# A multiply of the scan's inputs, from VectorE to GpSimd: a decoder layer with a selective scan on one core

## The chip, the cores and the metric

The kernel runs on one core of a Trainium2 chip. The metric is the device time of one execution in microseconds (us); lower is better. The engines are TensorE (PE in the profile, its weight loads PEld), VectorE (DVE), ScalarE (ACT), GpSimd (POOL) and SyncE (SP), which here only issues DMAs. SBUF and PSUM are the on-chip memories; GpSimd works on SBUF only.

## What is computed

One layer with three parts, each with a residual and a layer norm, for x of 4 batch rows x 512 positions x 512 channels, in float32. The change lies in the first part, a selective scan over 1024 inner channels (e) with 16 states (n) each:

```python
hidden = silu(conv(x @ W_in[:, :E]) + conv_bias)           # b, e, l
dt, Bm, Cm = split(hidden^T @ W_x, [128, 144])             # 128 + 16 + 16
dts = softplus(dt @ W_dt + b_dt)                           # b, l, e
dA  = exp(dts[..., None] * A)                              # b, l, e, n
dBu = dts[..., None] * Bm[:, :, None, :] * hidden[..., None]
state = dA[t] * state + dBu[t];  y[t] = sum_n state * Cm[t]
out = ((y + hidden * D) * silu(gate)) @ W_out
```

Behind it come an attention over a context (softmax) and a feed-forward product on values rounded to int8 range.

## The kernel before

Everything is written by hand for each engine, with semaphores between them. The batch rows are worked one after the other, each as 32 steps g (`STEPS`, with the row b from -1 to 4; -1 prepares row 0, 4 finishes row 3). A tile of 128 inner channels (8 per row) is scanned in four **units** of 32 channels x 4 states on the 128 partitions, each with 4 states more along the free axis (`NJ`). Step g of row b works unit u = 32 b + g + 1. Positions run along the free axis, 512 of them.

What a tile needs goes as follows. TensorE makes z = dt_s @ W_dt for the tile (item "z", at steps with g % 4 == 2, two tiles ahead: `Z_AT`). ScalarE's `soft` (L523 to L532) writes softplus of it to `steps[:, n % 3, 0]` and raises `s_dt`. `step_inputs` (L724 to L734) multiplies it with the convolved input `hs` into `steps[:, n % 3, 1]` and raises `s_du`. SyncE's `repeat` (L342 to L349) waits for `s_du` and copies 32 rows of both, four times over, into one of four `rep` buffers for each unit. From `rep`, ScalarE's `exps` make dA (four activations a unit, one unit ahead).

VectorE's `unit(u)` (L736 to L758) does two **products** dBu = rep * Bb, each 128x1024, from SBUF to PSUM (L747), then, at two units of lag (`DU_LAG`) behind the z item, the multiply `step_inputs` (L733), then two **scans** over dA in SBUF and dBu in PSUM (L755) into `st`. GpSimd's `weigh_states(u, h)` (L428 to L437) multiplies each half of the states with C, in place. Half 0 waits for the first scan of the unit. Half 1 waits for the second scan, and also for the products of the next unit and for the multiplies that stand behind them:

```python
if h and u + 1 < NB * UNITS:
    pool.wait_ge(s_mul, NH * (u + 2))
    pool.wait_ge(s_du, step_inputs_before(u + 2))
```

TensorE sums the weighted states of four units over partitions (`state_sum`, L886, at g % 4 == 0), VectorE's `finish` (L719) multiplies with the gate at g % 4 == 1. The products, attention and feed-forward of the row before are spread over the same steps (`REST`): layer-norm operations on VectorE (L700), small operations on GpSimd (L450, L452, and the bias add L461 of 128x512). `items(b, g)` lists the work of a step, and each engine goes through it in that order.

Of the kernel before, what the change touches and what calls it, by code (L numbers as in the profile page):

```python
# [5 lines left out]
ALU = mybir.AluOpType  # L6
# [11 lines left out]
NE = E // P  # L18
# [4 lines left out]
NQ = 4  # L23
# [3 lines left out]
UNITS = NE * NQ  # L27
TT = T // P
BANKS = 4
REPS = 4  # L30
# [27 lines left out]
SUM_AT = 0  # L58
FINISH_AT = 1
AHEAD = 4  # L60
DU_LAG = 2
NORM_LAG = 1
QUANT_LAG = 2

# [4 lines left out]
def items(b, g):  # L69

    keys = []
    after = b + 1 < NB
    n = NE * b + g // 4
    table = REST_AFTER if b == NB else REST

    def rest(kb, table, kinds):  # L80
        for kind in kinds:
            keys.extend((kind, kb, i) for i, at in enumerate(table.get(kind, ())) if at == g)

    if after and g == (B_AT if b >= 0 else 27):
        keys.extend(("sb", b + 1, j) for j in range(NJ))
    if after and b >= 0:
        keys.extend(("sc", b + 1, j) for j, at in enumerate(C_AT) if at == g)
    if (b, g) == (-1, 28):
        keys.extend(("sc", b + 1, j) for j in range(NJ))
    if b >= 1:  # L90
        rest(b - 1, table, ("wo", "q", "k", "at", "en"))
    if (g % 4 == Z_AT and 0 <= n + 2 < NB * NE and n != -1) or (b, g) == (-1, 28):
        keys.append(("z", (n + 2) // NE, (n + 2) % NE))
    if after and b >= 0:
        keys.extend(("c", b + 1, i) for i, at in enumerate(CONV_AT) if at == g)
    if after:
        keys.extend(("h", b + 1, i) for i, at in enumerate(HID_AT) if at == g)
    if b >= 1:
        rest(b - 1, table, ("xt", "av", "qt", "ff"))
    if b == LAST:  # L100
        rest(b, REST_BESIDE, ("q", "k", "at", "en", "wp"))
    if after and g == DT_AT:
        keys.append(("dt", b + 1, 0))
    if after and g == (BC_AT if b >= 0 else DT_AT):
        keys.append(("bc", b + 1, 0))

    if g % 4 == GATE_AT and 0 <= n < NB * NE:
        keys.append(("g", n // NE, n % NE))
    if b == 0 and g in (1, 2):
        keys += [("w", 0, 2 * (g - 1)), ("w", 0, 2 * (g - 1) + 1)]  # L110
    if b == 0 and g == 4:
        keys.append(("ws", 0, 0))
    if g % 4 == SUM_AT and 0 <= n - 1 < NB * NE:
        keys.append(("y", (n - 1) // NE, (n - 1) % NE))
    return keys


STEPS = [(b, g) for b in range(-1, NB + 1) for g in range(UNITS)]


def step_inputs_at(u):

    s = UNITS + u - 1 - DU_LAG
    return [key for key in items(*STEPS[s]) if key[0] == "z"] if u >= 1 else []


def step_inputs_before(u):

    return sum(key[0] == "z" for b, g in STEPS[:max(UNITS + u - 1 - DU_LAG, UNITS)] for key in items(b, g))


def norm_order():
# [4 lines left out]
def decoder_layer(nc, x, xT, ctxT, w_in, w_conv, conv_k, conv_b, w_x, w_dt, b_dt, w_out, a_log, d_skip,  # L137
# [9 lines left out]
    with ExitStack() as ctx:  # L147
# [28 lines left out]
        hs = sb("hs", [P, 2, NE, T])  # L176
        steps = sb("steps", [P, 3, 2, T])
# [77 lines left out]
        s_hs = sem("hs_ready")  # L255
# [154 lines left out]
        @block.gpsimd  # L410
        def _(pool):
            for dst in (ident, sel):
                nc.gpsimd.memset(dst[:], 0.0).then_inc(s_maskset, 1)
            nc.gpsimd.memset(ones[:], 1.0).then_inc(s_masks, 1)
            nc.gpsimd.memset(unround[:], -ROUND).then_inc(s_masks, 1)
            nc.gpsimd.memset(rounder[:], ROUND).then_inc(s_masks, 1)
            nc.gpsimd.memset(eps[:], EPS).then_inc(s_masks, 1)
            nc.gpsimd.memset(neghalf[:], -0.5).then_inc(s_maskset, 1)
            pool.wait_ge(s_maskset, 3)
            nc.gpsimd.affine_select(out=ident[:], in_=ident[:], compare_op=ALU.not_equal, fill=1.0,  # L420
                                    base=0, pattern=[[-1, P]], channel_multiplier=1).then_inc(s_masks, 1)

            for n, d in enumerate(range(-3, 4)):
                if n:
                    pool.wait_ge(s_masks, 5 + n)
                nc.gpsimd.affine_select(out=sel[:], in_=sel[:], compare_op=ALU.not_equal, fill=1.0,
                                        base=32 * d, pattern=[[-1, P]], channel_multiplier=1).then_inc(s_masks, 1)
            def weigh_states(u, h):  # L428

                spread_read(pool, "sc", u, h)  # L430
                pool.wait_ge(s_scan, NH * u + h + 1)
                if h and u + 1 < NB * UNITS:
                    pool.wait_ge(s_mul, NH * (u + 2))
                    pool.wait_ge(s_du, step_inputs_before(u + 2))
                j = slice(JH * h, JH * h + JH)
                s = st[:, u % RING, j, :]
                nc.gpsimd.tensor_tensor(s, s, Cb[:, j, :], ALU.mult).then_inc(s_p, 1)  # L437

            rows = []
            for b, g in STEPS:  # L440
                u = UNITS * b + g + 1
                scanned = 0 <= u < NB * UNITS
                if scanned:
                    weigh_states(u, 0)
                for key in rows:

                    n = norm[key]
                    c = slice(n % 4, n % 4 + 1)
                    pool.wait_ge(s_var, n + 1)
                    nc.gpsimd.tensor_tensor(rstd[:, c], var[:, c], neghalf[:], ALU.pow).then_inc(s_rstd, 1)  # L450
                    pool.wait_ge(s_rstd, 2 * n + 1)
                    nc.gpsimd.tensor_tensor(nmean[:, c], nmean[:, c], rstd[:, c], ALU.mult).then_inc(s_rstd, 1)  # L452
                rows = []
                for key in items(b, g):
                    kind, kb, i = key
                    if kind == "qt":

                        pool.wait_ge(s_xq, TT * kb + i + 1)
                        pool.wait_ge(s_bias, 16 * min(kb + 1, LAST))
                        x_i = rows_of[kb][:, i, :]  # L460
                        nc.gpsimd.tensor_tensor(x_i, x_i, bias_bc, ALU.add).then_inc(s_xb, 1)  # L461
                    if key in norm:
                        rows.append(key)
                if scanned:
                    weigh_states(u, 1)
# [211 lines left out]
        def _(dve):  # L677
# [43 lines left out]
                dve.wait_ge(s_y, NE * b + e + 1)  # L721
                dve.sem_inc(free, 1)  # L722

            def step_inputs(key):  # L724

                _, b, e = key
                n = NE * b + e
                dve.wait_ge(s_dt, n + 1)
                dve.wait_ge(s_hs, n + 1)
                if n >= 3:  # L730
                    for v in range(NQ * (n - 3), NQ * (n - 2)):
                        dve.wait_ge(s_rep[v % REPS], 64 * (v // REPS + 1))
                V.tensor_tensor(steps[:, n % 3, 1, :], steps[:, n % 3, 0, :], hs[:, b % 2, e, :],  # L733
                                ALU.mult).then_inc(s_du, 1)  # L734

            def unit(u):  # L736
                dve.wait_ge(s_rep[u % REPS], 64 * (u // REPS + 1))
                if u >= RING:

                    n = (u - RING) // NQ  # L740
                    product_done(dve, ("y", n // NE, n % NE))
                for h in range(NH):
                    j = slice(JH * h, JH * h + JH)
                    spread_read(dve, "sb", u, h)
                    if u:
                        dve.wait_ge(s_scan, NH * (u - 1) + h + 1)
                    V.tensor_tensor(dBu[:, j, :], rep[:, u % REPS, 1:2, :].to_broadcast([P, JH, T]), Bb[:, j, :],  # L747
                                    ALU.mult).then_inc(s_mul, 1)
                for key in step_inputs_at(u):
                    step_inputs(key)  # L750
                for h in range(NH):
                    j = slice(JH * h, JH * h + JH)
                    dve.wait_ge(s_mul, NH * u + h + 1)
                    dve.wait_ge(s_dA, NJ * u + JH * (h + 1))
                    V.tensor_tensor_scan(st[:, u % RING, j, :].rearrange("p j t -> p (j t)"),  # L755
                                         dA[:, u % 2, j, :].rearrange("p j t -> p (j t)"),
                                         dBu[:, j, :].rearrange("p j t -> p (j t)"), 0.0,
                                         ALU.mult, ALU.add).then_inc(s_scan, 1)  # L758
# [23 lines left out]
            for s, (b, g) in enumerate(STEPS):  # L782
                if 0 <= UNITS * b + g + 1 < NB * UNITS:
                    unit(UNITS * b + g + 1)
                if b == -1:
                    for key in items(b, g):
                        if key[0] == "z":
                            step_inputs(key)
                if b == -1 and g == HID_AT[-1] + 1:
                    quantize_weight()  # L790
                n = NE * b + g // 4 - 1
# [245 lines left out]
```

## Time and profile before

| | |
|---|---|
| median of 3 runs | 1140.06 us (1139.74 to 1140.76) |
| profiled execution | 1141.5 us, span 1139.7 us |
| TensorE busy | 855.1 us (75%) |
| VectorE busy | 1015.2 us (89%) |
| ScalarE busy | 775.5 us (68%) |
| GpSimd busy | 688.5 us (60%) |
| granted TensorE clock, mean | 0.886 |

The span runs from the first to the last instruction. Busy times are sums over each engine; "idle before" is the time in which an engine waited ahead of an instruction, with the instruction that ended it. "issue" means that the profile shows nothing that it waited for. Instructions of one engine overlap by some hundredths of a microsecond.

### The profile page before, as it was taken

Reading aid. Unit: us, or ns where it says so; the run is one execution under the profiler, and the core shown is the slowest. Engines: PE = TensorE matmul, PEld = TensorE weight load, DVE = VectorE, ACT = ScalarE, POOL = GpSimd, SP = SyncE. Lnnn points to the kernel's source line nnn. Section 1 sums busy time; section 2 is a strip of 40 time slices with the busy share of each in tenths; the row PEclk is TensorE's granted clock in tenths of the full one; section 3 lists DMA queues with packets and bytes.
Section 4 is the critical chain, followed back from the end, with each engine's and each line's share of the span. In section 5 each row is a group of like instructions: output and inputs, shape, how many; then the busy total and the mean of one; then the engine's idle time right before and its main releaser. Section 6 shows DMA issues by size and latency. Waiting matters only on the chain.

```text
span 1139.7 us, 10601 instructions
## 1 busy us (share of the span) xinstructions
PE 855.1 (75%) x2958; PEld 335.9 (29%) x2968; DVE 1015.2 (89%) x813; ACT 775.5 (68%) x1193; POOL 688.5 (60%) x387
## 2 busy tenths in 40 slices
PE   7944578884689689987669689897569557757884
PEld 3311133331134233432124234332124223322331
DVE  3589999999989987999999988999989999999823
ACT  3466566775766776886666786886657777777446
POOL 1046666666666665777667655587656767677423
PEclk9978799997789899999789899999779768888996
DMA  6163344453732443343743443254733353243000
GB/s 183 45 155 87 92 121 117 114 138 104 190 98 63 114 117 94 100 117 93 215 120 83 111 109 103 59 141 112 216 89 74 95 136 84 57 133 97 1 0 38
DMA packets 58427, 120.09 MB, mean 105 GB/s; under 512 B 12160, under 2 KB 18432, under 8 KB 58368
## 3 DMA queue, kind: packets, MB, share of 16 engines
q1 hardware_dynamic: 57648, 119.34, 40.3%
q8 instruction: 24, 0.39, 0.1%
q14 instruction: 35, 0.29, 0.1%
q10 hardware_dynamic: 720, 0.08, 0.0%
HBM read 48.07 MB, written 4.19 MB: 46 GB/s over the span
## 4 chain that ended last, share of the span: by engine, by line
issue 39%; DVE 31%; PE 20%; ACT 7%; POOL 1%; DMA 1%; DVEq 0%; ACTq 0%; SPq 0%; POOLq 0%
DVE st L755 21%; PE dense L854 11%; DVE dBu L747 3%; PE dense L909 3%; PE dense L886 2%; DVE x L700 2%; ACT dA L542 2%; PE dense L933 1%; DVE hs L719 1%; DVE steps L733 1%; ACT L530 1%; DVE xsc L806 1%; DVE dense L838 1%; ACT squares L566 1%; ACT L519 1%
## 5 line engine op out<-in xcount | busy, mean ns | idle before, releaser
L437 POOL TENSOR_TENSOR st<-st,Cb 128x1024 f32<-128x1024 f32 x256 | 597.3, 2355 | 405.5 <-issue 236.4
L755 DVE TENSOR_TENSOR_SCAN st<-dA,dBu 128x1024 f32<-128x1024 f32 x256 | 570.2, 2268 | 0.0
L542 ACT ACTIVATE dA<-rep,Aneg 128x511 f32<-128x511 f32 x512 | 329.2, 712 | 88.2 <-DVE st L755 86.4
L747 DVE TENSOR_TENSOR dBu<-rep,Bb 128x1024 f32<-128x1024 f32 x256 | 327.6, 1323 | 21.9 <-issue 7.3
L854 PE MATMUL dense<-xTs,Win 128*128 128x512 f32 x512 | 239.3, 612 | 16.6 <-DVEq L722 8.2
L886 PE MATMUL dense<-st,sel 128*32 128x512 f32 x1024 | 125.3, 628 | 32.7 <-POOL st L437 32.4
L854 PE MATMUL dense<-wide,hs 128*128 128x512 f32 x256 | 121.9, 633 | 31.6 <-issue 31.6
L854 PEld LDWEIGHTS dense<-xTs,Win 128*128 128x128 f32 x512 | 98.7, 196 | 147.7 <-issue 147.0
L909 PE MATMUL dense<-pj,Win 128*128 128x512 f32 (+1 forms) x192 | 97.3, 654 | 28.9 <-issue 13.1
L542 ACT ACT_TABLE_LOAD x62 | 79.5, 1283 | 12.8 <-DVE st L755 7.4
L871 PE MATMUL dense<-ident,small 128*128 128x128 f32 x112 | 22.4, 337 | 82.4 <-ACT small L584 55.5
L854 PEld LDWEIGHTS dense<-wide,hs 128*128 128x128 f32 x256 | 51.1, 204 | 100.6 <-issue 100.3
L886 PEld LDWEIGHTS dense<-st,sel 128*32 128x32 f32 x1024 | 30.2, 113 | 123.5 <-issue 76.5
L450 POOL TENSOR_TENSOR rstd<-var,neghalf 128x1 f32<-128x1 f32 x48 | 44.2, 921 | 37.0 <-ACT var L569 36.7
L933 PE MATMUL dense<-small,sel 128*32 128x512 f32 x256 | 38.2, 717 | 37.8 <-DVEq L722 35.1
L576 ACT ACTIVATE x<-x,nmean,rstd 128x512 f32<-128x512 f32 x36 | 29.1, 816 | 51.6 <-POOL nmean L452 51.3
L909 PEld LDWEIGHTS dense<-pj,Win 128*128 128x128 f32 x192 | 39.0, 212 | 85.2 <-issue 78.0
L854 PE MATMUL dense<-wide 128*128 128x512 f32 x96 | 46.5, 630 | 0.3 <-issue 0.3
L871 PEld LDWEIGHTS dense<-ident,small 128*128 128x128 f32 x112 | 15.7, 169 | 98.9 <-ACT small L584 63.3
L700 DVE SCALAR_TENSOR_TENSOR x<-dense,x 128x512 f32<-128x512 f32 x36 | 24.7, 686 | 22.0 <-PE dense L854 15.7
L854 PE MATMUL dense<-dt_s,Wdt 128*128 128x512 f32 x64 | 39.5, 702 | 3.5 <-ACT dt_s L547 2.0
L637 ACT ACTIVATE ta<-dense 128x512 f32<-128x512 f32 x32 | 19.1, 598 | 33.0 <-PE dense L854 32.4
(105 smaller groups left out, 772.9 us busy)
## 6 DMA issues: line engine op xcount, KB each, us to landing
rep<-steps SPq DMA_DIRECT2D x512, 128.0 KB, 2.4
Win<-w_in SPq DMA_DIRECT2D x64, 256.0 KB, 2.9
wide<-w_out SPq DMA_DIRECT2D x4, 2048.0 KB, 10.3
Win<-w_conv SPq DMA_DIRECT2D x24, 256.0 KB, 2.9
xTs<-xT SPq DMA_DIRECT2D x4, 1024.0 KB, 5.5
x<-x SPq DMA_DIRECT2D x3, 1024.0 KB, 8.9
out<-x SPq DMA_DIRECT2D x12, 256.0 KB, 2.0
wide<-w_x SPq DMA_DIRECT2D x4, 640.0 KB, 4.9
```

Of the source, the lines that this page charges most:

```text
L437: nc.gpsimd.tensor_tensor(s, s, Cb[:, j, :], ALU.mult).then_inc(s_p, 1)
L450: nc.gpsimd.tensor_tensor(rstd[:, c], var[:, c], neghalf[:], ALU.pow).then_inc(s_rstd, 1)
L542: nc.scalar.activation(dA[:, u % 2, j, 1:T], rep[:, u % REPS, 0, 1:T], ACT.Exp, scale=Aneg[:, u % UNITS, j:j + 1]).then_inc(s_dA, 1)
L576: nc.scalar.activation(x_i, x_i, ACT.Identity, scale=rstd[:, n % 4:n % 4 + 1], bias=nmean[:, n % 4:n % 4 + 1]).then_inc({"wo": s_ln1, "av" ...
L700: V.scalar_tensor_tensor(x_i, ps, 1.0, x_i, ALU.mult, ALU.add, accum_out=rowsum[:, n % 4:n % 4 + 1]).then_inc(s_sum, 1)
L747: V.tensor_tensor(dBu[:, j, :], rep[:, u % REPS, 1:2, :].to_broadcast([P, JH, T]), Bb[:, j, :], ALU.mult).then_inc(s_mul, 1)
L755: V.tensor_tensor_scan(st[:, u % RING, j, :].rearrange("p j t -> p (j t)"), dA[:, u % 2, j, :].rearrange("p j t -> p (j t)"), dBu[:, j, :] ...
L854: mm = nc.tensor.matmul(ps[0:rows, :], lhsT, rhs, start=n == 0, stop=n == len(pairs) - 1)
L871: mm = nc.tensor.transpose(ps[:, k * P:(k + 1) * P], src[:, k * P:(k + 1) * P], ident[:])
L886: mm = nc.tensor.matmul(ps[32 * q:32 * q + 32, :], sel[:, 0:32], st[:, (4 * n + q) % RING, j, :], start=False, stop=j == NJ - 1)
L909: mm = nc.tensor.matmul(ps[:, k:T], Win[:, n % 3, k, :], pj[:, 0:T - k], start=k == 0, stop=k == KC - 1)
L933: mm = nc.tensor.matmul(ps[32 * n:32 * n + 32, :], sel[:, row + n:row + n + 1].to_broadcast([P, 32]), bc_s, start=True, stop=True)
```

## The change

The multiply leaves VectorE's program. GpSimd does it in the step whose items hold the z, between its weighing of half 0 and of half 1 of that step's unit, and behind the norm operations that stand there in some steps. The wait for loads of `rep` that stood ahead of it and GpSimd's wait for `s_du` are gone.

```diff
-DU_LAG = 2
...
             def weigh_states(u, h):
...
                 if h and u + 1 < NB * UNITS:
                     pool.wait_ge(s_mul, NH * (u + 2))
-                    pool.wait_ge(s_du, step_inputs_before(u + 2))
...
                 for key in items(b, g):
                     kind, kb, i = key
-                    if kind == "qt":
+                    n = NE * kb + i
+                    if kind == "z":
+
+                        pool.wait_ge(s_dt, n + 1)
+                        pool.wait_ge(s_hs, n + 1)
+                        nc.gpsimd.tensor_tensor(steps[:, n % 3, 1, :], steps[:, n % 3, 0, :], hs[:, kb % 2, i, :],
+                                                ALU.mult).then_inc(s_du, 1)
+                    elif kind == "qt":
...
-            def step_inputs(key):
-
-                _, b, e = key
-                n = NE * b + e
-                dve.wait_ge(s_dt, n + 1)
-                dve.wait_ge(s_hs, n + 1)
-                if n >= 3:
-                    for v in range(NQ * (n - 3), NQ * (n - 2)):
-                        dve.wait_ge(s_rep[v % REPS], 64 * (v // REPS + 1))
-                V.tensor_tensor(steps[:, n % 3, 1, :], steps[:, n % 3, 0, :], hs[:, b % 2, e, :],
-                                ALU.mult).then_inc(s_du, 1)
...
-                for key in step_inputs_at(u):
-                    step_inputs(key)
```

GpSimd's order around the first z of the scanned part, before: the weighings of units 2 and 3 and of half 0 of unit 4. The waits in brackets are semaphores: `scan_done`, `dBu_done` (a product), `step_inputs_ready` (the multiply).

```order
L437 TENSOR_TENSOR st<-st,Cb 128x1024 [waits scan_done]
L437 TENSOR_TENSOR st<-st,Cb 128x1024 [waits step_inputs_ready,dBu_done,scan_done]
L437 TENSOR_TENSOR st<-st,Cb 128x1024 [waits scan_done]
L437 TENSOR_TENSOR st<-st,Cb 128x1024 [waits step_inputs_ready,dBu_done,scan_done]
L437 TENSOR_TENSOR st<-st,Cb 128x1024 [waits scan_done]
```

And with the change (`steps_ready` is softplus, `hs_ready` the convolved input):

```order
L424 TENSOR_TENSOR st<-st,Cb 128x1024 [waits scan_done]
L424 TENSOR_TENSOR st<-st,Cb 128x1024 [waits dBu_done,scan_done]
L424 TENSOR_TENSOR st<-st,Cb 128x1024 [waits scan_done]
L448 TENSOR_TENSOR steps<-steps,hs 128x512 [waits hs_ready,steps_ready]
L424 TENSOR_TENSOR st<-st,Cb 128x1024 [waits dBu_done,scan_done]
L424 TENSOR_TENSOR st<-st,Cb 128x1024 [waits scan_done]
```

The multiply stands between the two weighings of unit 3, ahead of the one that waits for the products of unit 4.

VectorE's order, units 4 and 5 and the products of unit 6, before:

```order
L747 TENSOR_TENSOR dBu<-rep,Bb 128x1024 [waits scan_done,rep_loaded0]
L747 TENSOR_TENSOR dBu<-rep,Bb 128x1024 [waits scan_done]
L755 SCALAR_TENSOR_TENSOR st<-dA,dBu 128x1024 [waits dA_ready,dBu_done] x2
L747 TENSOR_TENSOR dBu<-rep,Bb 128x1024 [waits scan_done,rep_loaded1]
L747 TENSOR_TENSOR dBu<-rep,Bb 128x1024 [waits scan_done]
L733 TENSOR_TENSOR steps<-steps,hs 128x512 [waits hs_ready,steps_ready]
L755 SCALAR_TENSOR_TENSOR st<-dA,dBu 128x1024 [waits dA_ready,dBu_done] x2
```

With the change:

```order
L729 TENSOR_TENSOR dBu<-rep,Bb 128x1024 [waits scan_done,rep_loaded0]
L729 TENSOR_TENSOR dBu<-rep,Bb 128x1024 [waits scan_done]
L735 SCALAR_TENSOR_TENSOR st<-dA,dBu 128x1024 [waits dA_ready,dBu_done] x2
L729 TENSOR_TENSOR dBu<-rep,Bb 128x1024 [waits scan_done,rep_loaded1]
L729 TENSOR_TENSOR dBu<-rep,Bb 128x1024 [waits scan_done]
L735 SCALAR_TENSOR_TENSOR st<-dA,dBu 128x1024 [waits dA_ready,dBu_done] x2
```

The multiply between the products and the scans of unit 5 is gone; it now stands in GpSimd's order one unit and a half earlier.

## Rows read from the trace of the kernel before

**Rows 1.** The page: busy time, share of the span and instructions of each engine.

```profile
PE 855.1 (75%) x2958; PEld 335.9 (29%) x2968; DVE 1015.2 (89%) x813; ACT 775.5 (68%) x1193; POOL 688.5 (60%) x387
```

**Rows 2.** Stretches: length, busy PE, PEld, DVE, ACT, POOL (count), clock, DMA share, GB/s.

```profile
150.00:300.00 150.00, 115.95 (x422) 40.96 (x421) 148.78 (x93) 99.39 (x133) 95.94 (x42) 0.92 0.51 133
```

**Rows 3.** Groups by form, VectorE: busy us, mean ns, then idle us before them.

```profile
L755 DVE TENSOR_TENSOR_SCAN st<-dA,dBu 128x1024 f32<-128x1024 f32 x256 | 570.2, 2268 | 0.0
L747 DVE TENSOR_TENSOR dBu<-rep,Bb 128x1024 f32<-128x1024 f32 x256 | 327.6, 1323 | 21.9 <-issue 7.3 <-DVE x L700 7.1 <-PE dense L886 3.8
L733 DVE TENSOR_TENSOR steps<-steps,hs 128x512 f32<-128x512 f32 x32 | 21.8, 682 | 8.4 <-ACT steps L530 8.4
```

**Rows 4.** Timeline, VectorE, 200 to 232 us: start us, duration us, instruction, count.

```profile
200.01 2.37 DVE L747 TENSOR_TENSOR dBu<-rep,Bb 128x1024 f32<-128x1024 f32 x2 [0.24 <-DVE hs L719]
202.29 4.46 DVE L755 TENSOR_TENSOR_SCAN st<-dA,dBu 128x1024 f32<-128x1024 f32 x2
206.66 2.73 DVE L747 TENSOR_TENSOR dBu<-rep,Bb 128x1024 f32<-128x1024 f32 x2
209.30 4.45 DVE L755 TENSOR_TENSOR_SCAN st<-dA,dBu 128x1024 f32<-128x1024 f32 x2
...
216.92 4.45 DVE L755 TENSOR_TENSOR_SCAN st<-dA,dBu 128x1024 f32<-128x1024 f32 x2
...
229.26 2.37 DVE L747 TENSOR_TENSOR dBu<-rep,Bb 128x1024 f32<-128x1024 f32 x2 [0.24 <-DVE hs L719]
```

**Rows 5.** Timeline, GpSimd, the same stretch.

```profile
202.51 4.65 POOL L437 TENSOR_TENSOR st<-st,Cb 128x1024 f32<-128x1024 f32 x2 [2.92 <-issue]
209.52 4.66 POOL L437 TENSOR_TENSOR st<-st,Cb 128x1024 f32<-128x1024 f32 x2 [2.36 <-issue]
217.17 4.67 POOL L437 TENSOR_TENSOR st<-st,Cb 128x1024 f32<-128x1024 f32 x2 [2.99 <-DVE steps L733]
```

**Rows 6.** Line 747 alone: durations in ns, shortest, median, longest.

```profile
L747 DVE TENSOR_TENSOR dBu<-rep,Bb x256: 1216/1228/1706, 62.0 to 1079.1; 128x1024 f32<-128x1024 f32 x128
```

**Rows 7.** Timeline, 455 to 500 us: two product pairs on VectorE, then GpSimd.

```profile
458.07 2.74 DVE L747 TENSOR_TENSOR dBu<-rep,Bb 128x1024 f32<-128x1024 f32 x2
...
470.35 2.37 DVE L747 TENSOR_TENSOR dBu<-rep,Bb 128x1024 f32<-128x1024 f32 x2 [0.24 <-DVE x L700]
...
458.53 1.54 POOL L450 TENSOR_TENSOR rstd<-var,neghalf 128x1 f32<-128x1 f32 x1
460.15 0.70 POOL L452 TENSOR_TENSOR nmean<-nmean,rstd 128x1 f32<-128x1 f32 x1
460.81 1.26 POOL L461 TENSOR_TENSOR x<-x,small 128x512 f32<-128x512 f32 x1
462.04 4.66 POOL L437 TENSOR_TENSOR st<-st,Cb 128x1024 f32<-128x1024 f32 x2
```

**Rows 8.** Timeline, ScalarE: softplus at three of the 30 places.

```profile
201.87 0.69 ACT L530 ACTIVATE steps<-dense,bdt 128x512 f32<-128x512 f32 x1
...
297.35 0.69 ACT L530 ACTIVATE steps<-dense,bdt 128x512 f32<-128x512 f32 x1
...
390.72 0.69 ACT L530 ACTIVATE steps<-dense,bdt 128x512 f32<-128x512 f32 x1
```

**Rows 9.** Timeline, GpSimd, near the second and third of these.

```profile
297.29 4.68 POOL L437 TENSOR_TENSOR st<-st,Cb 128x1024 f32<-128x1024 f32 x2 [2.36 <-issue]
...
390.91 4.65 POOL L437 TENSOR_TENSOR st<-st,Cb 128x1024 f32<-128x1024 f32 x2 [2.35 <-issue]
```

**Rows 10.** Timeline, VectorE: products and waits between 395 and 435 us.

```profile
395.65 2.35 DVE L747 TENSOR_TENSOR dBu<-rep,Bb 128x1024 f32<-128x1024 f32 x2
...
406.85 2.37 DVE L747 TENSOR_TENSOR dBu<-rep,Bb 128x1024 f32<-128x1024 f32 x2 [3.25 <-issue]
...
433.37 0.69 DVE L700 SCALAR_TENSOR_TENSOR x<-dense,x 128x512 f32<-128x512 f32 x1 [5.08 <-PE dense L854]
```

More of the change, by code:

```diff
@@ L118 @@
 STEPS = [(b, g) for b in range(-1, NB + 1) for g in range(UNITS)]
[L121 to L129, printed above, removed]
 def norm_order():
@@ L784, in _ @@
                     unit(UNITS * b + g + 1)
[L785 to L788, printed above, removed]
                 if b == -1 and g == HID_AT[-1] + 1:
```

## The prediction

> **What bounds the kernel now.** I read the page's busy times first. VectorE is busy for 1015 of 1139.7 us, GpSimd for 689 [rows 1]. The share alone would make every instruction taken off VectorE a gain. The table of stretches says the same of the first of the four batch rows, where little but the scan runs: from 150 to 300 us VectorE is busy for 148.8 of 150 us and GpSimd for 95.9 [rows 2]. The groups by form give the price of one: a scan 2.268 us, a product 1.323 us on average, the multiply that is to be moved 0.682 us, 32 of them [rows 3].
>
> The timelines say what the share hides. A unit is two products, then two scans. Its period is 7.01 us (scans start at 202.29 and at 209.30) [rows 4]. GpSimd weighs the states of two halves in 4.65 us, and starts 0.2 us behind the last product [rows 5]. Two scans take 4.37 us (202.29 to 206.66), so GpSimd's pair ends at 207.16, half a microsecond after VectorE has started on the next product. That pair of products takes 2.73 us, where the pair at 200.01, with GpSimd at rest, takes 2.37 us [rows 4]. All 256 products lie between 1.216 and 1.706 us, and half take 1.228 or less [rows 6]: a product is held while GpSimd still works. So the period is GpSimd's pair plus two products, 4.65 + 2.23 + 0.13 = 7.01, and not VectorE's own 2.28 + 4.37 = 6.65. The scans (0.0 us idle before them, mean 2.268 us [rows 3]) are not slowed beside GpSimd; the products are. The scan reads one operand from SBUF and one from PSUM, the product reads both from SBUF, and so does the moved multiply.
>
> The other way round it holds too. At 458.53 GpSimd's tiny rstd operation ran into two products and took 1.54 us; nmean, behind it, took 0.70 us, until the second product ended at 460.81 (458.07 + 2.74). The operation behind that, 128x512 with both inputs in SBUF and so the form of the moved one, ran beside a scan, took 1.26 us, and the next began 1.23 us after it [rows 7]. rstd ended before the second product did: GpSimd gets its turn between two products. The Trainium skill says this as a rule (SBUF — State Buffer, "Who interferes with whom"): a VectorE instruction with two SBUF inputs contends with a GpSimd instruction that reads SBUF, and the later one waits for the whole of the other. By that rule the sum is the one below; the trace agrees, with 2.73 against 2.37 us. By a sharing of bandwidth, which the rows do not fit, it would be that of the first rival.
>
> **The change, part by part.** Removed from VectorE: 32 multiplies, 30 of them in the scanned part. The scans of a unit that holds one start 7.62 us after those of the unit before (209.30 to 216.92), not 7.01 [rows 4]. Each is worth 0.61 us, since GpSimd's pair waits for it too: GpSimd starts at 217.17, its idle time put down to the steps multiply [rows 5].
>
> Added to GpSimd: the same 32, at 1.23 us of its time each [rows 7]. The place decides. In unit u with g % 4 == 2 the multiply stands between the two weighings of that unit, so it can run only when VectorE has begun on the products of u + 1. If GpSimd takes its turn at once or between the products, the second or both products wait 1.23 us; if it waits for both, its own pair starts 1.23 us late and holds the products of u + 2. Either way the ring of pair and products grows by 1.23 us. Against 0.61 taken away: +0.62 us.
>
> Its inputs: softplus ends at 202.56 (201.87 + 0.69) [rows 8], the first weighing of the unit at 207.16; no wait. I went through the 30 places in the timelines:
> - 13 like this one, all 7 of the first batch row among them. In three of them softplus ends inside the first product, which gives the same turn. 13 x 0.62 = +8.1 us.
> - 3 at the last such step of a batch row. Softplus ends at 298.04 (297.35 + 0.69) [rows 8]; GpSimd could have gone on at 297.29 [rows 9]. Behind the multiply it goes on at 299.34, 2.05 us later: 3 x (2.05 - 0.61) = +4.3 us. What is queued behind this wait is the weighing, and the next products wait for that.
> - 3 at the tenth step. Softplus ends at 391.41 [rows 8], GpSimd went on at 390.91 [rows 9]: it would at 392.7, end at 397.3, and hold the product of 395.65 [rows 10] by 1.7 us, net 1.1. In two of the three VectorE soon waits 3.25 us for TensorE anyway (at 406.85) [rows 10]: nothing. The third: +1.1 us.
> - 3 in which GpSimd's norm operations stand ahead: the multiply lands beside the scans, the pair ends 0.8 us past the next product's start: +0.2 each, +0.6 us.
> - 2 ahead of VectorE's wait of 5.08 us for TensorE (at 433.37) [rows 10], which swallows the 1.23. Only the removal counts: -1.2 us.
> - 6 behind norm operations, beside a scan, like the 1.26 us operation of [rows 7]. There GpSimd's pair starts at 462.04 and ends at 466.7, and the next product is only at 470.35 [rows 7, 10]. In four that room covers 1.23 us (-0.61 each, -2.4); in two it is 0.3 us, and +0.35 each is left (+0.7).
>
> The sum is 8.1 + 4.3 + 1.1 + 0.6 - 1.2 - 2.4 + 0.7 = +11.2 us.
>
> Costed at nothing: the two multiplies ahead of the scans (0.6 us longer on GpSimd, but the first scan waits for ScalarE's exps, which stand behind the second softplus); GpSimd's wait for the multiply, dropped, since its wait for the products remains; the waits for loads that VectorE made ahead of the multiply. SyncE's repeats, four DMAs a unit, wait for the multiply; it now comes some 8 us earlier (about 208.5 where it was at 216.3 to 217.0), so the repeats and the weight loads queued behind them are issued no later, perhaps a unit earlier. They found VectorE's products waiting for nothing there, so I take no gain; if the weights come earlier for TensorE, a microsecond or two may come back at its waits.
>
> What the trace does not show is a 128x512 operation on GpSimd against a product. Bounds: nothing, if the two can share (0 in place of 1.23), and 2.46, if the multiply first waits for a product, leaves GpSimd's order late by it, and then holds the next as well. I take 1.23, as rows 4 and 7 both show one-at-a-time, with no further loss in the handover (2.23 + 4.65 + 0.13 already fills the 7.01).
>
> [...]
>
> **The rivals.** *Faster.* The second operand's path is wide enough for both when GpSimd's operation is short; the products keep to about 1.23 us beside the moved multiply, and VectorE simply loses its work. For it: 99% busy VectorE [rows 2], and GpSimd has 2.36 us between its pairs [rows 5], more than 1.26. Against: 2.73 against 2.37 us, and the 1.54 us rstd. It decides at the length of the product beside the multiply: below about 1.8 us the change wins. Worth 28 x -0.61 = -17.1 (all but the two that a wait swallows), less 6.2 for the late softplus (3 x 2.05) and 1.7 at one tenth step, so about -9: 1131 us.
>
> *Slower by much.* No place has room: every multiply costs 0.62 (30 x 0.62 = 18.6) and the late softplus another 3 x 0.8 + 3 x 0.5 = 3.9; that is +22.5, 1163 us. For it: a delay at one place moves ScalarE's exps and the following softplus, so the room I found in the timeline may be used up. Against: VectorE's waits of 3 to 5 us for TensorE in two batch rows.
>
> *Slower by little.* The waits for TensorE of the second and third batch row swallow more than I gave them; then the first row and the boundaries remain, 7 x 0.62 + 1.4 = +5.8, 1146 us.
>
> *No change.* The multiply is on GpSimd but its 1.23 us hides behind something I read as tight, so that it cancels 0.61 on average: 1140 us. Against: a place with room 0.61 is not found in the first batch row.
>
> **How the numbers follow.** The profiled execution took 1141.5 us (span 1139.7), 1.4 above the median 1140.06. 1141.5 + 11.2 = 1152.7; on the median's scale 1151.3. A measurement of this kernel tells some 0.2% (2.3 us) from no change. Chances: forecast (+8 to +15) 0.62; slower by much 0.13; slower by little 0.12; no change 0.05; faster 0.08. So faster 0.08, same 0.05, slower 0.87. The range leaves out the faster and the no-change case and the far end of the large one: 1144 to 1159.
>
> **What would show it.** In the changed profile: 32 operations of 128x512 on GpSimd, 1.26 us or, where they wait for a product, up to 2.4; products of up to 2.5 us, 13 or more of them over 1.75; units of 8.2 us in place of 7.01 at every fourth, and none of 7.62; in the first batch row +0.6 us in each group of four (29.25 to 29.85). GpSimd idle ahead of its multiply for ScalarE's softplus in about six places. VectorE's busy time rises, though it has 32 instructions less. I am wrong if no product exceeds 1.75 us, or if the group of four units falls to about 28.6 us.

## The result and the profile after

The changed kernel takes 1150.48 us (median of 5 runs, 1148.49 to 1151.65), the kernel before 1140.06 (1139.12 to 1141.61). The ratio is 1.009, 95% interval 1.0079 to 1.0101. It is slower by some 10.4 us. The profiled execution is the shortest of the five (1148.49 us, span 1146.6), and that of the kernel before lay 1.4 us above its median (1141.5, span 1139.7). So the two traces show 6.9 us of the 10.4 in the span.

The page's busy times, against [rows 1]:

```profile
PE 850.6 (74%) x2958; PEld 334.1 (29%) x2968; DVE 1024.8 (89%) x781; ACT 774.3 (68%) x1193; POOL 747.7 (65%) x419
```

VectorE has 32 instructions less and is busy for 9.6 us more. The page's groups, against [rows 3], say which ones grew (busy us, mean ns, idle before):

```profile
L735 DVE TENSOR_TENSOR_SCAN st<-dA,dBu 128x1024 f32<-128x1024 f32 x256 | 570.1, 2267 | 2.0 <-ACT dA L536 2.0
...
L729 DVE TENSOR_TENSOR dBu<-rep,Bb 128x1024 f32<-128x1024 f32 x256 | 356.2, 1435 | 29.1 <-DMA rep<-steps 7.5
...
L448 POOL TENSOR_TENSOR steps<-steps,hs 128x512 f32<-128x512 f32 x32 | 55.2, 1726 | 83.4 <-ACT steps L524 83.3
```

The scans are as before. The products took 327.6 us in all and take 356.2, which is 28.6 more; the 21.8 us of the multiply are gone. GpSimd's multiply takes 1.726 us on average, where its own time is 1.26. The stretch from 150 to 300 us, against [rows 2], has the same VectorE busy time to the hundredth, which shows how little that number tells:

```profile
150.00:300.00 150.00, 116.16 (x417) 40.58 (x416) 148.78 (x87) 97.02 (x131) 103.60 (x45) 0.91 0.51 133
```

The timeline from 200 to 232 us, VectorE and then GpSimd, against [rows 4, 5]:

```profile
201.63 2.37 DVE L729 TENSOR_TENSOR dBu<-rep,Bb 128x1024 f32<-128x1024 f32 x2 [0.24 <-DVE hs L713]
203.91 4.46 DVE L735 TENSOR_TENSOR_SCAN st<-dA,dBu 128x1024 f32<-128x1024 f32 x2
208.28 3.81 DVE L729 TENSOR_TENSOR dBu<-rep,Bb 128x1024 f32<-128x1024 f32 x2
212.01 4.45 DVE L735 TENSOR_TENSOR_SCAN st<-dA,dBu 128x1024 f32<-128x1024 f32 x2
216.38 2.77 DVE L729 TENSOR_TENSOR dBu<-rep,Bb 128x1024 f32<-128x1024 f32 x2
219.07 4.45 DVE L735 TENSOR_TENSOR_SCAN st<-dA,dBu 128x1024 f32<-128x1024 f32 x2
...
231.37 2.37 DVE L729 TENSOR_TENSOR dBu<-rep,Bb 128x1024 f32<-128x1024 f32 x2 [0.24 <-DVE hs L713]
...
204.14 4.65 POOL L424 TENSOR_TENSOR st<-st,Cb 128x1024 f32<-128x1024 f32 x2 [2.91 <-DVE dBu L729]
208.75 2.25 POOL L448 TENSOR_TENSOR steps<-steps,hs 128x512 f32<-128x512 f32 x1
212.24 4.69 POOL L424 TENSOR_TENSOR st<-st,Cb 128x1024 f32<-128x1024 f32 x2 [1.24 <-DVE dBu L729]
```

GpSimd's multiply stands ready at 208.75, waits for the first product, and takes its turn before the second: 2.25 us, 1.26 of them its own. The pair of products takes 3.81 us in place of 2.73. From scan to scan that unit is 8.10 us (203.91 to 212.01) where it was 7.01, and the unit that held the multiply on VectorE is 7.06 (212.01 to 219.07) where it was 7.62. From the products at 201.63, the first behind a `finish`, to those behind the next, at 231.37, a group of four units takes 29.74 us, against 29.25 [rows 4].

At the first row boundary the late softplus shows, and something that I had not foreseen (timeline of the changed kernel, ScalarE, GpSimd and VectorE):

```profile
300.43 0.69 ACT L524 ACTIVATE steps<-dense,bdt 128x512 f32<-128x512 f32 x1
...
301.19 1.27 POOL L448 TENSOR_TENSOR steps<-steps,hs 128x512 f32<-128x512 f32 x1 [3.18 <-ACT steps L524]
302.41 5.69 POOL L424 TENSOR_TENSOR st<-st,Cb 128x1024 f32<-128x1024 f32 x2
...
304.52 4.67 DVE L729 TENSOR_TENSOR dBu<-rep,Bb 128x1024 f32<-128x1024 f32 x2
```

GpSimd idles for 3.18 us until softplus is there. Its pair then starts so late that a product waits already when the first weighing ends, and goes ahead of the second. Pair and products are interleaved: 5.69 us for the pair, 4.67 for the products.

Laid side by side, scan by scan, the changed kernel's trace stands against that of before at -0.2 us at the first scan (at 64.2 us before), +3.1 at the last of row 0, +4.9 and +6.7 at the last of rows 1 and 2, and +7.3 at the last scan of all. So the trace shows 7.5 us in the scanned part.

### The profile page after: what moved, and what is told of

Its sections match the earlier page's. It is cut to its first block, busy times and chain, and to the rows that moved or that the text cites. A ratio compares the mean times of both kernels' runs of the same rounds, so it can differ in the third digit from the quotient of the medians.

```text
span 1146.6 us, 10543 instructions
## 1 busy us (share of the span) xinstructions
PE 850.6 (74%) x2958; PEld 334.1 (29%) x2968; DVE 1024.8 (89%) x781; ACT 774.3 (68%) x1193; POOL 747.7 (65%) x419
## 4 chain that ended last, share of the span: by engine, by line
issue 38%; DVE 29%; PE 24%; ACT 6%; POOL 2%; DMA 1%; DVEq 0%; ACTq 0%; SPq 0%; POOLq 0%
DVE st L735 20%; PE dense L830 14%; PE dense L885 4%; DVE dBu L729 3%; PE dense L862 3%; DVE x L694 1%; DVE hs L713 1%; POOL st L424 1%; PE dense L909 1%; ACT dA L536 1%; PE dense L856 1%; DVE xsc L782 1%; DVE dense L814 1%; ACT squares L560 1%; PE dense L847 1%
## 5 line engine op out<-in xcount | busy, mean ns | idle before, releaser
L729 DVE TENSOR_TENSOR dBu<-rep,Bb 128x1024 f32<-128x1024 f32 x256 | 356.2, 1435 | 29.1 <-DMA rep<-steps 7.5
L862 PE MATMUL dense<-st,sel 128*32 128x512 f32 x1024 | 128.9, 643 | 38.1 <-POOL st L424 38.1
L830 PE MATMUL dense<-wide,hs 128*128 128x512 f32 x256 | 119.3, 622 | 36.4 <-issue 35.6
L448 POOL TENSOR_TENSOR steps<-steps,hs 128x512 f32<-128x512 f32 x32 | 55.2, 1726 | 83.4 <-ACT steps L524 83.3
L437 POOL TENSOR_TENSOR rstd<-var,neghalf 128x1 f32<-128x1 f32 x48 | 49.7, 1035 | 42.8 <-ACT var L563 42.8
```

The lines of the kernel that those rows point to most:

```text
L448: nc.gpsimd.tensor_tensor(steps[:, n % 3, 1, :], steps[:, n % 3, 0, :], hs[:, kb % 2, i, :], ALU.mult).then_inc(s_du, 1)
L830: mm = nc.tensor.matmul(ps[0:rows, :], lhsT, rhs, start=n == 0, stop=n == len(pairs) - 1)
L862: mm = nc.tensor.matmul(ps[32 * q:32 * q + 32, :], sel[:, 0:32], st[:, (4 * n + q) % RING, j, :], start=False, stop=j == NJ - 1)
```

## The experiments

Each total is a median, with its ratio to the kernel before as run beside it: 1139.66 us for the first four, 1140.1 us for the others.

**E1: the multiply two steps later.** GpSimd multiplies at the same place between two weighings, but for the z of two steps ago, as VectorE did.

```diff
+                for key in items(*STEPS[STEPS.index((b, g)) - 2]) if b >= 0 else items(b, g):
+                    if key[0] == "z" and (b < 0 or NE * key[1] + key[2] >= 2):
+                        step_inputs(key)
                 for key in items(b, g):
                     kind, kb, i = key
-                    n = NE * kb + i
-                    if kind == "z":
...
-                    elif kind == "qt":
+                    if kind == "qt":
```

> GpSimd's multiply stays between the two weighings of a unit, but of the unit two steps later, so that softplus is long done. Theory (one of the two at a time: the products and GpSimd's multiply both read two operands from SBUF): a group of four units in the first batch row stays at 29.7 us and the second product at about 2.3 us, the wait for softplus at the row boundaries goes, three times +1.3 us become +0.5, total 1147 to 1150 us. Rival (the cost is the wait for a late softplus, with the weighing queued behind it): nearly all of the 10 us goes, 1141 us or less.

Measured 1143.09 us, ratio 1.0029 (1.0018 to 1.0041). The first row did what the theory said: each group of four units gains 0.6 us for the multiply gone from VectorE and loses 1.05 to 1.25 us at GpSimd's turn. Two product pairs of it, an ordinary one and the one that holds the turn, and GpSimd's multiply:

```profile
154.80 2.73 DVE L732 TENSOR_TENSOR dBu<-rep,Bb 128x1024 f32<-128x1024 f32 x2
...
161.82 3.87 DVE L732 TENSOR_TENSOR dBu<-rep,Bb 128x1024 f32<-128x1024 f32 x2
...
162.34 2.26 POOL L420 TENSOR_TENSOR steps<-steps,hs 128x512 f32<-128x512 f32 x1
```

But the total lies between the two expectations and inside neither: 7 us of the 10.4 hang on when GpSimd asks for softplus and where in the dense steps (those that also carry the work of the row before) it multiplies; this run moves both and does not separate them. I had given the late softplus three.

**E2: the multiply beside the scans.** It stands behind the second weighing of its step, so no product is running when it starts.

```diff
-                    if kind == "z":
...
-                    elif kind == "qt":
+                    if kind == "qt":
...
                 if scanned:
                     weigh_states(u, 1)
+                for key in items(b, g):
+                    if key[0] == "z":
+                        step_inputs(key)
```

> GpSimd's multiply is put behind the second weighing of the step, so it runs beside the scans and meets no product. Theory (GpSimd's pair and the two products form a ring that has no room): the multiply no longer interrupts a pair of products, but the next products wait for the pair, 1.6 in place of 0.4 us; the group of four units in the first row stays at 29.6 to 29.8 us, total 1147 to 1151 us. Rival (the cost lies only in the place between two products): group 28.6 us, total 1125 to 1133 us.

Measured 1150.03 us, ratio 1.0091 (1.0078 to 1.0105). Its timeline in the first row, VectorE and GpSimd:

```profile
202.29 2.37 DVE L733 TENSOR_TENSOR dBu<-rep,Bb 128x1024 f32<-128x1024 f32 x2 [0.24 <-DVE hs L717]
...
215.97 3.99 DVE L733 TENSOR_TENSOR dBu<-rep,Bb 128x1024 f32<-128x1024 f32 x2
...
232.17 2.37 DVE L733 TENSOR_TENSOR dBu<-rep,Bb 128x1024 f32<-128x1024 f32 x2 [0.24 <-DVE hs L717]
...
211.83 2.35 POOL L431 TENSOR_TENSOR st<-st,Cb 128x1024 f32<-128x1024 f32 x1 [2.37 <-DVE dBu L733]
214.13 1.27 POOL L420 TENSOR_TENSOR steps<-steps,hs 128x512 f32<-128x512 f32 x1
215.36 2.37 POOL L431 TENSOR_TENSOR st<-st,Cb 128x1024 f32<-128x1024 f32 x1
```

The multiply meets no product and takes 1.27 us, and yet the group grows to 29.88 us (202.29 to 232.17), 0.14 more than in the changed kernel. What it delays is the second weighing, which ends at 217.73; so the pair of products of 215.97 takes 3.99 us. So the place between two products is not what costs. The ring of weighings and products has no room in the first row, wherever the multiply stands in it.

**E3: no multiply.** Ones, written once at the start, stand in its place, so this kernel leaves the factor out (as E4 does).

```diff
-                V.tensor_tensor(steps[:, n % 3, 1, :], steps[:, n % 3, 0, :], hs[:, b % 2, e, :],
-                                ALU.mult).then_inc(s_du, 1)
+                dve.sem_inc(s_du, 1)
...
+            link(V.memset(steps[:, :, 1, :], 1.0))
```

> The multiply is left out on every engine (ones stand in its place, so the scan's input is not the reference's); VectorE only signals. It sizes the term that the change removes. Theory: 0.61 us for each of 28 to 30, group of four units 28.64 us, total 1122 to 1125 us. Rival (the removed multiply was hidden, since the ring of GpSimd and products sets the period): under 5 us gained, 1135 us or more.

Measured 1125.84 us, ratio 0.988 (0.9865 to 0.9894). From one `finish` to the next, in the first row:

```profile
196.21 2.37 DVE L746 TENSOR_TENSOR dBu<-rep,Bb 128x1024 f32<-128x1024 f32 x2 [0.24 <-DVE hs L719]
...
224.82 2.37 DVE L746 TENSOR_TENSOR dBu<-rep,Bb 128x1024 f32<-128x1024 f32 x2 [0.24 <-DVE hs L719]
```

The group is 28.61 us, 0.64 less than before, 0.60 of it in the unit that held the multiply. In all it is 13.8 us, not 17: VectorE's waits for TensorE in rows 1 and 2 swallow some of it.

**E4: GpSimd only writes.** The changed kernel, with a memset in the place of the multiply.

```diff
-                        nc.gpsimd.tensor_tensor(steps[:, n % 3, 1, :], steps[:, n % 3, 0, :], hs[:, kb % 2, i, :],
-                                                ALU.mult).then_inc(s_du, 1)
+                        nc.gpsimd.memset(steps[:, n % 3, 1, :], 1.0).then_inc(s_du, 1)
```

> GpSimd writes ones with a memset of 128x512 in the place of its multiply: it stands in the same place of its order with the same waits, but reads nothing from SBUF. The scan's input is not the reference's. Theory (the reads take turns): no product over 1.75 us beside it, group of four units 28.6 to 28.7 us, total 1122 to 1127 us, near the kernel without the multiply plus the late softplus. Rival (any work of GpSimd there holds the product): a second product of 1.23 us plus the memset's time, group over 28.9 us.

Measured 1130.92 us, ratio 0.9919 (0.9904 to 0.9933). Its timeline at the place where the multiply took 2.25 us:

```profile
203.99 2.73 DVE L728 TENSOR_TENSOR dBu<-rep,Bb 128x1024 f32<-128x1024 f32 x2
...
204.43 0.53 POOL L448 MEMSET steps<- 128x512 f32 x1
```

It runs inside the products, waits for nothing, and the pair stays at 2.73 us, so the theory's first half holds. It is also what the Trainium skill says (SBUF — State Buffer, "Who interferes with whom"): a VectorE instruction with two SBUF inputs does not contend with a GpSimd one that only writes; this trace agrees, with 0.53 us and 2.73. The total is 4 us above the expectation, and 5.1 above E3. Scan by scan the excess sits where GpSimd waits for softplus. At the three row boundaries the trace has +0.70, +0.73 and +0.71 us against that of before, where E3 has -0.6 each; at the three tenth steps it has some +0.2, where E3 has -0.6 each, and a part of that difference is gone a unit later. Eight products are over 1.75 us in this run (up to 2.94). None stands in the first row's ordinary units; six stand at these late places, where the weighing holds them that was queued behind the wait.

**E5 and E6: products with one operand from SBUF**, with the multiply on VectorE (E5, from the kernel before) and on GpSimd (E6, from the changed one). The factor from `rep` is left out.

```diff
-                    V.tensor_tensor(dBu[:, j, :], rep[:, u % REPS, 1:2, :].to_broadcast([P, JH, T]), Bb[:, j, :],
-                                    ALU.mult).then_inc(s_mul, 1)
+                    V.tensor_scalar(dBu[:, j, :], Bb[:, j, :], 0.5, None, ALU.mult).then_inc(s_mul, 1)
```

> The kernel before, with every product reading one operand from SBUF (Bb times a constant; the factor from rep is left out), its waits kept. The multiply is on VectorE. Theory (only instructions with two operands from SBUF take turns with GpSimd): no product is held, none over 1.3 us; the period falls from 7.01 to about 6.65 us, VectorE's own sum, group of four units about 28.1 us, total 1105 to 1120 us. Rival (products are held by GpSimd for another reason, such as GpSimd's writes or the wait on semaphores): products up to 1.7 us stay, group 29.2 us.

> The changed kernel with the same product of one operand. Theory: GpSimd's multiply and the product run side by side (multiply 1.26 us, none near 2.25), and the change now gains in the first row: group 27.5 us, 0.6 less than in the run with the multiply on VectorE; in total 8 to 14 us below that run, the late softplus taking back some 5. Rival (the multiply costs for being on GpSimd, not for the shared operands): 5 to 12 us above that run, as in the pair with full products.

E5 measured 1116.96 us, ratio 0.9797 (0.9785 to 0.981). Its timeline, VectorE and GpSimd: the pair that starts while GpSimd still works takes 2.33 us, and the group is 27.97 us.

```profile
193.88 2.35 DVE L747 TENSOR_SCALAR dBu<-Bb 128x1024 f32<-128x1024 f32 x2 [0.25 <-DVE hs L719]
...
200.52 2.33 DVE L747 TENSOR_SCALAR dBu<-Bb 128x1024 f32<-128x1024 f32 x2
...
221.85 2.35 DVE L747 TENSOR_SCALAR dBu<-Bb 128x1024 f32<-128x1024 f32 x2 [0.25 <-DVE hs L719]
...
196.37 4.66 POOL L437 TENSOR_TENSOR st<-st,Cb 128x1024 f32<-128x1024 f32 x2 [2.89 <-issue]
```

E6 measured 1102.03 us, ratio 0.9665 (0.9652 to 0.9677), 14.9 us below E5. Its timeline:

```profile
190.36 2.35 DVE L729 TENSOR_SCALAR dBu<-Bb 128x1024 f32<-128x1024 f32 x2 [0.24 <-DVE hs L713]
...
197.00 2.33 DVE L729 TENSOR_SCALAR dBu<-Bb 128x1024 f32<-128x1024 f32 x2
...
217.73 2.35 DVE L729 TENSOR_SCALAR dBu<-Bb 128x1024 f32<-128x1024 f32 x2 [0.25 <-DVE hs L713]
...
197.47 1.28 POOL L448 TENSOR_TENSOR steps<-steps,hs 128x512 f32<-128x512 f32 x1
```

The same multiply in the same place of GpSimd's order now takes 1.28 us in the middle of a pair that takes 2.33, and the group is 27.37 us, 0.60 below E5. One operand of one instruction (its opcode changes with it) turns the change from a loss of 10.4 into a gain of 14.9 us. The multiply has the same length and the same place on GpSimd in both, so neither the engine nor its load is what costs, but reads that take turns. The totals hold a second effect of the same kind: GpSimd's weighings no longer hold the products either, which gives the ring room. The gain lies above the 14 us I had put at the top, since with that room the late softplus costs nothing: at the three row boundaries E6 is 0.60 us below E5, as in the other units that held a multiply.

**E7: only the wait.** The kernel before, multiply on VectorE, with the changed kernel's wait on GpSimd.

```diff
                     kind, kb, i = key
+                    if kind == "z":
+                        pool.wait_ge(s_dt, NE * kb + i + 1)
                     if kind == "qt":
```

> The kernel before with the multiply on VectorE, and one wait more: GpSimd waits for softplus of the step, where the changed kernel would multiply. Theory as it stands after the runs with a later multiply and with a memset: the wait alone delays GpSimd's next weighing at three row boundaries by 0.7 to 1.3 us and at three tenth steps by 0.2, in all 3 to 5 us, 1142.5 to 1145 us. Rival (the wait costs nothing by itself, the 7 us between the two lags are a matter of where GpSimd's multiply meets products): within 1 us of the kernel before.

Measured 1147.46 us, ratio 1.0058 (1.0045 to 1.0072), or +7.4. The order of things is right and the size was again too small. At the boundary, GpSimd and VectorE:

```profile
297.16 4.69 POOL L437 TENSOR_TENSOR st<-st,Cb 128x1024 f32<-128x1024 f32 x2 [3.18 <-ACT steps L532]
...
300.49 3.59 DVE L749 TENSOR_TENSOR dBu<-rep,Bb 128x1024 f32<-128x1024 f32 x2
```

GpSimd waits 3.18 us ahead of its weighing, as in the changed kernel ahead of its multiply, and the next pair takes 3.59 us in place of 2.75: +0.84 there, and +0.86 and +0.84 at the other two. The rest is spread: +0.1 at each group of the first row, +0.4 at the tenth step of the last row (in rows 1 and 2 the next unit takes it back), +0.7 at the sixteenth steps of rows 1 and 2, and in row 2 +1.0 us at a wait of VectorE for TensorE. The profiled execution shows 5.9 us from the first scan on; I have not followed the rest.

**E8: nine of the 32 on GpSimd.** In E1's trace the multiplies of the steps 6, 14 and 18 of rows 1 to 3 cost nothing. Only those go to GpSimd, at the old lag of two steps, and GpSimd's wait for the multiply counts only VectorE's.

```diff
+ON_POOL = [(b, g) for b in (1, 2, 3) for g in (6, 14, 18)]
...
-    return [key for key in items(*STEPS[s]) if key[0] == "z"] if u >= 1 else []
+    return [key for key in items(*STEPS[s]) if key[0] == "z" and STEPS[s] not in ON_POOL] if u >= 1 else []
...
+                if STEPS[STEPS.index((b, g)) - DU_LAG] in ON_POOL:
+                    for key in items(*STEPS[STEPS.index((b, g)) - DU_LAG]):
+                        if key[0] == "z":
+                            step_inputs(key)
```

> GpSimd does the multiply at 9 of the 32 places, two steps behind the z items of steps 6, 14 and 18 of rows 1 to 3, where in the run with a later multiply it stood beside scans and held nothing; VectorE does the other 23 as before. Theory: -0.6 us at each of the nine, less what VectorE's waits for TensorE swallow, -3 to -5.5 us: 1134 to 1137 us, below both kernels. Rival (every multiply on GpSimd costs somewhere in the ring): 1139 us or more.

Measured 1134.16 us (1131.95 to 1135.22), ratio 0.9946 (0.9934 to 0.9958): faster than both kernels. Its groups by form, GpSimd's multiply and VectorE's products:

```profile
L763 DVE TENSOR_TENSOR dBu<-rep,Bb 128x1024 f32<-128x1024 f32 x256 | 327.1, 1321 | 21.9 <-DVE x L716 7.4 <-issue 6.5 <-PE dense L902 4.6
...
L437 POOL TENSOR_TENSOR steps<-steps,hs 128x512 f32<-128x512 f32 x9 | 11.4, 1268 | 0.0
```

None of the nine waits (1.268 us on average), and the products are at 1.321 us on average, as in [rows 3].

The nine places do not earn all of it. The trace gains 6.5 us from the first scan to the last, and the units from which a multiply was taken, with those behind them, hold between 3 and 4. Some 3.7 us come in three units of the last row that lost no multiply, where VectorE's waits got shorter. The longest of these, before and in E8:

```profile
854.33 0.69 DVE L700 SCALAR_TENSOR_TENSOR x<-dense,x 128x512 f32<-128x512 f32 x1 [3.35 <-issue]
...
850.91 0.69 DVE L716 SCALAR_TENSOR_TENSOR x<-dense,x 128x512 f32<-128x512 f32 x1 [1.95 <-issue]
```

Why these waits shrank was not followed. So the size of the gain, unlike its sign, is partly luck.

## Why the prediction was right, point by point

It gave 1151.3 us, in 1144 to 1159, and 1150.48 was measured. The mechanism is shown; that the total is so near is partly luck. The sum of +11.2 us was made from one trace, and in the traces the scanned part grew by 7.5 us. Group by group of the 30 places, in the order of the prediction, the scans moved by +5.0 (for +8.1), +4.0 (+4.3), +1.4 (+1.1), -0.5 (+0.6), -1.4 (-1.2) and -1.1 us (-1.7, which is -2.4 and +0.7). That is +7.4. The medians differ by 10.4 us, as the executions profiled lie above the median before and below it after; where the other 3 us lie, no trace shows.

- **The turn between products.** Right in kind: E4 takes the read away and the product is free, E5 and E6 take the product's second operand away and the sign turns. In size 1.23 us was too much: the unit grows by 1.09 (8.10 against 7.01). It is 1.25 where the multiply runs beside the scans (E2, group +0.63, with 0.61 taken off). The prediction had the ring grow by 1.23 us either way.
- **The multiply taken off VectorE, 0.61 us.** Right: 0.60 in E3's first row. So an ordinary group of four in the first row grows by 0.49 us, not 0.62, and the whole row by 3.3 us, for 4.3 in the sum.
- **"3 at the last such step of a batch row", +1.44 each.** +1.31, +1.34 and +1.31 us. The size is near, the way there not: I had the whole pair 2.05 us late, and instead a product slips between the two weighings.
- **"3 at the tenth step", nothing twice and +1.1 once.** +1.0 in the last row, as said. In the other two the scans also come 1.0 us later, and the wait behind them gives back 0.65 and 1.0.
- **"13 like this one."** Three of these, in which softplus ends inside the first product, cost nothing together (-0.24, +0.55, -0.32 net) in place of 0.62 each. VectorE stands before them in a wait for TensorE that got shorter. At the first, before and after:

```profile
326.22 0.69 DVE L700 SCALAR_TENSOR_TENSOR x<-dense,x 128x512 f32<-128x512 f32 x1 [2.45 <-PE dense L854]
...
329.90 0.69 DVE L694 SCALAR_TENSOR_TENSOR x<-dense,x 128x512 f32<-128x512 f32 x1 [1.73 <-PE dense L830]
```

- **The late softplus as a term.** Over an ordinary turn the sum held some 3 us for it (3 x 0.8 and once 0.5). At these places that was right: E7's trace has three times 0.85 and once 0.4. What was missed lies elsewhere. The wait alone costs 7.4 us in E7, 5.9 of them in its trace, and 3.0 of these come at places where the prediction had nothing for it; E4 against E3 gives 5.1. How much of this acts in the changed kernel is not shown.
- **The turns as a term.** The sum held 1.23 us at nearly every place, some 25 us in all (an estimate, from 13 x 1.23, 4 x 1.23, 3 x 0.81 and 2 x 0.96). The changed kernel against E4 (+10.4 and -8.7 us from the kernel before) has 19 us, and that includes what the multiply takes longer on GpSimd than the memset (1.26 against 0.53 us). This error and that of the softplus have opposite signs.
- **"SyncE's repeats ... no gain."** Not tested by itself. SyncE waited 257.4 us in all for the multiply before and 28.9 us after, and its waits for the products rose from 275.8 to 434.5 us in turn: the queue is held by the next thing in it.
- **The rival "faster"** was to be recognized by a product of less than 1.8 us beside the multiply. The pair of 3.81 us, its second product 2.30, rules it out, and E6 shows under which condition it would have been right: products that read one operand from SBUF.
- **What the profile was to show** came: multiplies of up to 2.27 us, one unit of 8.1 in four, 22 products over 1.75 us, VectorE's busy time higher with fewer instructions. Two counts were off. "Idle ahead of its multiply in about six places" was nine in the scanned part, and "products of up to 2.5 us" was 3.4 at the three row boundaries, where a whole weighing (2.35 us) stands ahead of the second product:

```profile
L729 DVE TENSOR_TENSOR dBu<-rep,Bb x256: 1216/1232/3398, 59.6 to 1086.4; 128x1024 f32<-128x1024 f32 x128
```

In the balance of the runs: -13.8 us for the multiply taken off VectorE (E3), +5.1 for GpSimd's wait and order (E4 against E3), +19 for the reads that take turns and the longer instruction (the change against E4). These are steps of one chain of runs, so that they add up to +10.4 confirms nothing by itself.

## What to carry to other kernels

Before moving an elementwise operation from VectorE to GpSimd, count the operands that it and VectorE's neighbouring instructions read from SBUF. Then find the ring that the two engines form through their turns: where it sets the pace, its period, not the busy share, is what a moved instruction adds to. Moving only those instructions that find GpSimd's pair with room behind it gave 0.5% (part of it from waits elsewhere), where moving all of them cost 0.9%. An added wait is priced by what is queued behind it on its engine at every place where it is late, not only at the three where it is plain to see.

## What the runs showed of the hardware

- A GpSimd operation that waits gets its turn between two products that VectorE issues back to back; in the other direction a waiting product goes between two weighings that GpSimd issues back to back (the 5.69 us pair at 302.41).
- With one operand less from SBUF, the product itself is hardly shorter (1.215 us on average in E5, against 1.228, the median in [rows 6]); some 20 of the 23 us from the kernel before to E5 come from not waiting, since 256 x 0.013 us is 3.3 (an estimate from these rows).
- GpSimd's multiply costs the ring 0.16 us more beside the scans (1.25, E2) than between two products (1.09, the changed kernel), in the first row; why was not followed.
